# Another order on VectorE, GpSimd and ScalarE in a cross-attention and FFN kernel: maximum and residual earlier, statistics of x later

## What is computed

```python
x = x + xattn(layernorm(x), ctx, Wq, Wk, Wv, Wskip)   # einsum over channels, softmax over 256
x = x + ffn(layernorm(x), qweight, scales, zeros, bias)

# xattn: q = Wq up; k = Wk down; v = Wv down; energy = q^T k / sqrt(128)
#        x = softmax(energy) v^T; returns Wskip up + x
# ffn:   w = (nibbles - round(zeros / scales)) * scales; returns x w + bias   (1024 by 1024)
```

## Time and profile before

| what | value |
|---|---|
| median of 3 runs | 538.35 us (537.58 to 538.68) |
| profiled execution, its own time | 536.69 us |
| its span in the profile | 534.9 us |
| mean granted clock of TensorE | 0.987 |
| busy share of the span | PE 94%, DVE 80%, ACT 69%, POOL 82% |
| HBM traffic | 23.87 MB read, 16.78 MB written |
| DMA hardware queue's packets | 79.9% of 16 engines' span |

### The profile page before, as it was taken

One profiled execution on the slowest core, in us unless ns is written; L12 is line 12 of the kernel. 1 busy time (PEld: TensorE's weight loads), 2 busy tenths in 40 slices (PEclk: granted clock), 3 DMA queues, 4 the chain that ended last, 5 costly groups with the idle time before them and its releaser, 6 DMA issues.

```text
span 534.9 us, 9272 instructions
## 1 busy us (share of the span) xinstructions
PE 505.3 (94%) x2700; PEld 311.9 (58%) x2700; DVE 429.2 (80%) x980; ACT 369.7 (69%) x844; POOL 436.4 (82%) x651
## 2 busy tenths in 40 slices
PE   5657999999999999999999999999999999999976
PEld 4544565656666665666665656666665666665532
DVE  6898788889888888888888889888888888877631
ACT  4877777776777767677777776767767677776510
POOL 5998788889888888988888889888888988888751
PEclk9888999999999999999999999999999999999998
DMA  8636888898788898888898788888897888876852
GB/s 319 172 88 115 144 191 179 179 184 186 168 150 206 188 178 178 181 189 153 178 204 163 193 185 181 157 192 178 172 196 177 194 171 173 163 142 143 154 113 78
DMA packets 236787, 91.65 MB, mean 171 GB/s; under 512 B 219200, under 2 KB 223808, under 8 KB 236736
## 3 DMA queue, kind: packets, MB, share of 16 engines
q1 hardware_dynamic: 236016, 90.92, 79.9%
q10 hardware_dynamic: 720, 0.14, 0.1%
HBM read 23.87 MB, written 16.78 MB: 76 GB/s over the span
## 4 chain that ended last, share of the span: by engine, by line
POOL 44%; PE 29%; issue 12%; ACT 5%; DVE 5%; DMA 3%; SPq 1%; POOLq 0%; ACTq 0%
PE ps_y L907 14%; POOL sb_prob L255 10%; POOL sb_xc_lo L270 9%; POOL sb_xn_lo L297 9%; POOL sb_o L249 6%; PE ps_e L861 5%; PE ps_o L891 4%; ACT sb_xn L487 4%; POOL sb_nb L281 3%; PE ps_o L887 2%; POOL sb_rstd L279 2%; DMA sb_xnt_lo<-sb_xn_lo 2%; POOL sb_rstd L263 2%; PE ps_kv L872 1%; PE ps_y L911 1%
## 5 line engine op out<-in xcount | busy, mean ns | idle before, releaser
L907 PE MATMUL ps_y<-sb_wf,sb_xnt_hi 128*128 128x512 f16 x512 | 196.9, 385 | 7.4 <-DMA sb_xnt_lo<-sb_xn_lo 4.0
L907 PE MATMUL ps_y<-sb_wf,sb_xnt_lo 128*128 128x512 f16 x512 | 196.0, 383 | 0.0
L469 ACT ACTIVATE sb_prob<-ps_e,sb_neg_max 128x256 f32<-128x256 f32 x256 | 117.8, 468 | 53.2 <-DVE sb_neg_max L647 53.2
L255 POOL TENSOR_SCALAR sb_prob<-sb_prob,sb_rsum 128x256 f32<-128x256 f32 x256 | 122.8, 493 | 4.2 <-DVE sb_rsum L652 4.2
L656 DVE TENSOR_TENSOR sb_p_lo<-sb_prob,sb_p_hi 128x1024 f16<-128x1024 f32 x64 | 78.0, 1220 | 48.0 <-ACT sb_p_hi L478 48.0
L297 POOL TENSOR_TENSOR sb_xn_lo<-sb_xn,sb_xn_hi 128x512 f16<-128x512 f32 x64 | 76.0, 1206 | 44.0 <-ACT sb_xn_hi L496 44.0
L861 PE MATMUL ps_e<-sb_k_hi,sb_xc_hi 128*128 128x256 f32 x256 | 85.4, 334 | 10.1 <-DVE sb_k_lo L635 5.5
L907 PEld LDWEIGHTS ps_y<-sb_wf,sb_xnt_hi 128*128 128x128 f16 x512 | 50.2, 98 | 72.8 <-issue 14.1
L478 ACT ACTIVATE sb_p_hi<-sb_prob 128x1024 f16<-128x1024 f32 x64 | 67.3, 1052 | 34.4 <-issue 30.0
L249 POOL TENSOR_TENSOR sb_o<-sb_prod,sb_x 128x512 f32<-128x512 f32 x64 | 80.8, 1281 | 9.5 <-DVE sb_prod L690 9.5
L647 DVE TENSOR_REDUCE sb_neg_max<-ps_e 128x2 f32<-128x512 f32 x128 | 84.8, 681 | 1.6 <-PE ps_e L861 1.2
(11 more groups left out here) (113 smaller groups left out, 917.7 us busy)
## 6 DMA issues: line engine op xcount, KB each, us to landing
sb_x<-in_x_dram SPq DMA_DIRECT2D x32, 512.0 KB, 4.3
out_dram<-sb_o SPq DMA_DIRECT2D x64, 256.0 KB, 2.3
sb_ctx<-in_ctx_dram SPq DMA_DIRECT2D x32, 128.0 KB, 2.8
sb_q<-in_L_ffn_qweight_dram SPq DMA_DIRECT2D x4, 512.0 KB, 7.1
sb_seed_l<-sb_rs SPq DMA_DIRECT2D x96, 0.5 KB, 2.2
sb_pt_hi<-sb_p_hi SPq DMA_TRANSPOSE x64, 4.1
sb_pt_lo<-sb_p_lo SPq DMA_TRANSPOSE x64, 3.4
sb_scale_row<-in_L_ffn_scales_dram SPq DMA_DIRECT2D x1, 512.0 KB, 9.3
```

The source lines that it names most:

```text
L255: last = pool.tensor_scalar(prob[:, j, t, :], prob[:, j, t, :], rsum[:, j, t:t + 1], P_SCALE, ALU.mult, ALU.mult)
L469: done = act.activation(prob[:, j, t, :], ps_e[j % 2][:, t, :], ACT.Exp, bias=neg_max[:, j, t:t + 1], accum_out=esum[:, j, t:t + 1])
L907: pe.matmul(ps_y[h][:, :], xnt_p[s][:, par, kt, :], wf[:, kt, h * HALF:(h + 1) * HALF], start=kt == 0 and s == 0, stop=False)
```

## The change

DVE does the fourth row maximum and the second residual earlier: the two low parts of keys and values move behind the third inversion, both halves of the second statistics stand together behind the fourth maximum, and the first layer norm's statistics of x(m) move from the head of the step to just before the last `probs_lo`. In step 2 `seed_rows` moves ahead and `nibbles(3)` falls behind with `values_lo`. POOL gets `inverse_std2` ahead of the fourth normalisation as before, but the second half of the low centred x now comes behind that normalisation, and `inverse_std1(m)` after it. ACT does the last exponentials before the first half of `probs_hi`. The low centred x gets one semaphore for each half: PE's first scores wait for the first half alone, and the third chunk of scores for the second.

```diff
@@ gpsimd: centred_lo @@
-                last = pool.tensor_tensor(xc_lo[:, n % 3, cols], xc[:, cols], xc_hi[:, n % 3, cols].bitcast(F32),
-                                          ALU.subtract)
-                if h == HALVES - 1:
-                    last.then_inc(xclo_done, 1)
+                pool.tensor_tensor(xc_lo[:, n % 3, cols], xc[:, cols], xc_hi[:, n % 3, cols].bitcast(F32),
+                                   ALU.subtract).then_inc(xclo_done[h], 1)
@@ gpsimd: step @@
                 if ran(b):
                     normalise(b, 0)
+                if ran(n):
+                    centred_lo(n, 0)
+                if ran(b):
+                    normalise(b, 1)
+                    normalise(b, 2)
+                if ran(a):
+                    inverse_std2(a)
+                if ran(b):
+                    normalise(b, 3)
+                if ran(n):
+                    centred_lo(n, 1)
                 if ran(m):
                     inverse_std1(m)
-                if ran(n):
-                    centred_lo(n, 0)
-                if ran(b):
-                    normalise(b, 1)
-                    normalise(b, 2)
-                if ran(n):
-                    centred_lo(n, 1)
-                if ran(a):
-                    inverse_std2(a)
-                if ran(b):
-                    normalise(b, 3)
@@ scalar: step @@
                     exps(b, 2)
+                    exps(b, 3)
                     probs_hi(b, 0)
-                    exps(b, 3)
@@ vector: step @@
                     value_scale(n)
-                if ran(m):
-                    stats1(m, 0)
-                    stats1(m, 1)
-                    aggregate1(m)
                 if ran(b):
                     invert(b, 0)
-                if ran(m):
-                    variance1(m)
                 if ran(a):
                     residual(a, 0)
                 if ran(b):
                     row_max(b, 1)
                     row_max(b, 2)
+                if t == 2:
+                    seed_rows()
+                if ran(b):
+                    invert(b, 1)
+                if ran(a):
+                    residual(a, 1)
+                if ran(b):
+                    invert(b, 2)
+                    row_max(b, 3)
                 if ran(a):
                     stats2(a, 0)
-                if ran(b):
-                    invert(b, 1)
+                    stats2(a, 1)
+                    aggregate2(a)
+                if ran(b):
+                    invert(b, 3)
                 if ran(n):
                     keys_lo(n)
                     values_lo(n)
                 if t == 2:
                     nibbles(3)
-                    seed_rows()
-                if ran(b):
-                    invert(b, 2)
-                if ran(a):
-                    residual(a, 1)
-                if ran(b):
-                    row_max(b, 3)
-                if ran(a):
-                    stats2(a, 1)
-                    aggregate2(a)
-                if ran(b):
-                    invert(b, 3)
+                if ran(b):
                     probs_lo(b, 0)
                 if ran(m):
                     context_max(m)
                 if ran(q):
                     scale_product(q, 0)
+                if ran(m):
+                    stats1(m, 0)
+                    stats1(m, 1)
+                    aggregate1(m)
+                    variance1(m)
                 if ran(b):
                     probs_lo(b, 1)
@@ tensor: scores @@
+                if j == 2:
+                    pe.wait_ge(xclo_done[1], b + 1)
@@ tensor: keys_ready @@
                 pe.wait_ge(klo_done, b + 1)
-                pe.wait_ge(xclo_done, b + 1)
+                pe.wait_ge(xclo_done[0], b + 1)
```

More of the change, by code:

```diff
@@ L109, in xattn_ffn_program @@
         w_step, w_scaled, proj_done, proj_kept = sem("w_step"), sem("w_scaled"), sem("proj_done"), sem("proj_kept")
-        key_done, key_kept, k0_done, xchi0_done, xclo0_done = (sem(n) for n in ("key", "key_kept", "k0", "xchi0", "xclo0"))
+        key_done, key_kept, k0_done, xchi0_done = (sem(n) for n in ("key", "key_kept", "k0", "xchi0"))
         k1_done, recip_done = sem("k1"), sem("recip")
@@ L115, in xattn_ffn_program @@
         st1_done, mv1_done, ve1_done, rstd1_done = (sem(n) for n in ("st1", "mv1", "ve1", "rstd1"))
-        xc_done, xchi_done, xclo_done = (sem(n) for n in ("xc", "xchi", "xclo"))
+        xc_done, xchi_done, xclo_done = sem("xc"), sem("xchi"), sems("xclo", HALVES)
         amax_done, kv_done, t_step, kvhi_done, kvlo_done = (sem(n) for n in ("amax", "kv", "t_step", "kvhi", "kvlo"))
@@ L386, in step @@
                     normalise(b, 0)
-                if ran(m):
-                    inverse_std1(m)
                 if ran(n):
@@ L399, in step @@
                     normalise(b, 3)
+                if ran(n):
+                    centred_lo(n, 1)
+                if ran(m):
+                    inverse_std1(m)
                 if ran(a):
@@ L422, in centre @@
                 if ran(n, 1):
-                    act.wait_ge(xclo_done, n)
+                    act.wait_ge(xclo_done[1], n)
                 act.activation(xc[:, :], x_sb[:, n % 4, :], ACT.Identity, bias=mv1[:, 0:1],
@@ L627, in first_centred_lo @@
                 done = dve.tensor_tensor(xc_lo[:, 0, cols], xc[:, cols], xc_hi[:, 0, cols].bitcast(F32), ALU.subtract)
-                done.then_inc((xclo0_done, xclo_done)[h], 1)
+                done.then_inc(xclo_done[h], 1)
             def keys_lo(n):
@@ L915, in keys_ready @@
                 pe.wait_ge(klo_done, b + 1)
-                pe.wait_ge(xclo_done, b + 1)
+                pe.wait_ge(xclo_done[0], b + 1)
             def run_in():
-                pe.wait_ge(klo_done, 1)
-                pe.wait_ge(xclo0_done, 1)
+                keys_ready(0)
                 scores(0, 0)
@@ L925, in run_in @@
                 second_keys()
-                pe.wait_ge(xclo_done, 1)
                 scores(0, 2)
```

## The result

| | before | after |
|---|---|---|
| median of 7 runs each | 537.70 us (537.26 to 538.68) | 539.75 us (539.38 to 540.99) |
| ratio, 95% interval | | 1.0037 [1.0025, 1.0049] |
| profiled execution, its span | 536.69 us, 534.9 us | 540.99 us, 539.2 us |

What follows compares the result with a forecast made beforehand. PE's 15.37 us step was taken as the floor, beside POOL's 15.42 us loop costing 0.8 us. Step 2 +1.0, steady steps +3.4 and end +1.2 gave +5.6: median 538.35 to 543.9 us, range 538.9 to 549.5.

Steps and rivals of the forecast that it cites:

- Part 1: Steady steps, DVE's new order: `probs_lo(b,1)` ends about 1 us after next scores 0 start, delaying transposes; net +3.4 us.
- the nine stands: Steady steps with a long `xn_hi` transpose issue: PE waits 0 to 1.2 us each, 4.2 us in all.
- rival A: Long issues no longer fall on the transposes, no stands; only step 2 and end cost: +0.4 to +1.4 us, chance 0.14.
- part 4: Low centred x, semaphore by halves: PE's first scores need only the first half; 0 to -0.15 us.
- Part 2: POOL's new order, steady steps: 15.42 us loop gone, worth 0.8 us; `xn_lo` ready 3.3 to 4.1 us after scores 0.
- The hold of 0.2: Steady steps: POOL's normalisation holds DVE's `probs_lo(b,0)`, so `probs_lo(b,1)` ends 0.2 us later; 0 to 0.5 possible.
- Parts 3 and 4: ACT's last exponentials first: nothing, or up to 1 us a step if uncovered; semaphore by halves: 0 to -0.15 us.
- Part 5: Step 2: first FFN starts early, stands about 4.6 us, half clock falls where PE bounds; +1.0 us, bounds -0.15 and +1.7.
- Part 6: Last steps: `stats2` now stands in the second layer norm's chain, 0.6 us twice; +1.2 us, ends 0.6 and 1.6.
- Both ends: Step 2, where the half clock falls later, +1.0 us, and the last steps' longer layer norm chain, +1.2 us.

Runs made afterwards that it cites:

- the middle alone: Changed kernel with the new order in steps 3 to 30 only, old order in step 2 and from step 31: 535.74 us, ratio 0.9973.
- the ladder: New order in steps 3 to 30 (0.9973), then new end (1.0008), then step 2 (1.0037); other way, step 2 before the end: 0.9973, 1.0028, 1.0037.

## Why the prediction was wrong

- **Part 1, the steady steps: this step failed.** Forecast +3.4 net, measured -0.7 in the profile and -1.0 to -1.45 by the middle alone. Its first half held: `probs_lo(b,1)` ends at T'+1.04 (1.0 worked out, without the 0.2 taken for a hold). Its second half, the nine stands of 4.2 us in all, did not: PE lost 0.2 us. "In the nine steps with the long issue" took these issues as fixed to the string; they belong to 16 KB transfers of instructions, and the one PE wait that part 4 adds, whose effect on them was put at nothing, moved those out of the string. That is rival A's condition, word for word, held at 0.14. By the profiles this move is worth 1.3 us. The larger part of the error is the price: with the transfers left on the string the stands came to 1.5, not 4.2. 2.4 of the 4.2 were put on two steps, those of the stands at 345 us and behind it, because they "had no room at all". What had used up the room in the first was the drift of `probs_lo(b,1)` to T'+0.85 by POOL's loop, together with a landing of 4.10 us; in the second, where it ended at T'+0.16, it was a long issue with a landing of 4.01. Part 2 ends that drift, so part 1 counted a lateness that part 2 takes away and put its own microsecond on top. And in the changed kernel `xn_lo` lands within 3.6 us from sequence 3 to 28, and 0.4 us of each long issue is taken up by SP's pause.
- **The hold of 0.2.** DVE was not held: `probs_lo` takes 1.21 to 1.22 us in the steady steps. POOL was (the mean of its 256 normalisations went from 493 to 616 ns). The Trainium skill has this rule (SBUF — State Buffer, section Who interferes with whom): the pair of ports goes for a whole instruction to whoever issues first. The trace agrees in the length of the hold, and in the order for `inverse_std1`, which begins 0.16 us behind `probs_lo` and takes 1.46. In the other case it doesn't show the order: by the records the normalisation begins at 382.49, 0.06 us ahead of `probs_lo` (382.55), and is held all the same.
- **Part 2** was right in each statement: the loop gone, the wait for `ve1` in place of that for `xn_hi`, `xn_lo` ready at T'+4.1, the upper of its bounds. It was priced too low: 0.8 by the stands of one profiled execution, which was itself 1.0 us under its median. The middle alone won 1.45 and POOL's order alone 1.9, or 1.0 to 1.1 and 1.5 to 1.9 among runs of the same mean clock. What the rest over 0.8 is, stands that the profiled execution of before did not show or something else, is open.
- **Parts 3 and 4** cost nothing by themselves that the profile shows, but for what part 4 did to the transfers.
- **Part 5, step 2: mechanism right, term mis-sized.** +1.0 forecast, 1.3 to 1.6 by the ratios (3.0 on one way of the ladder), 2.9 in the profile. The bound of +1.7 assumed that the half clock lasts 3.4 us; it lasted 6.8 in the profiled execution after and 3.4 in four kernels with a like stand. At 3.4 it cost about 1.5, within the bound; at 6.8, 2.8. What makes the difference is open.
- **Part 6, the end: right** by the profile, +1.2 forecast and 1.4 (1.0 against the kernel with the old end) measured; the ratios give 0.5 to 1.9 and hardly bound it.
- **The sum.** Both ends together 2.2 forecast, 3.4 measured; the middle +3.4 forecast, -1.45 measured: 5.6 + 1.2 - 4.85 = 2.0, the result. That the sign came out right is luck in so far: the loss is that of the ends, not that of the part that carried the forecast. Rival A had the mechanism and nearly the sum (+0.4 to +1.4), with -0.8 in the middle.

## What to carry to other kernels

A long DMA issue that comes back every few steps has a cause of its own, and before it is added to a moved string it must be found: look at what else the queues carry in that stretch. When an engine's start is moved forward while its last input is not, the stand moves too, and with it the place where the clock is low; ask first whether the last input can come earlier, which here was worth more (4 us and more) than the whole reordering. And try each engine's order alone: here POOL's by itself gave 0.9964, and all three together 1.0037. Before a stand is added to a step that already had one, find out what made the first, and whether the change takes it away.

## What was not expected of the hardware

- A transfer of instructions of 16 KB that meets a DMA transpose of 256 KB makes its issue take up to 2.5 us instead of 1.23 to 1.28 (2.0 to 2.5 in most cases). The transfers keep to PE's count of instructions, and one satisfied wait more per step of PE is enough to move them through a step (nine long issues of one transpose to two).
- Behind a stand of 4.7 us of PE the clock was at half for 6.8 us in one execution and 3.4 in four others. With 32 idle matmuls in the stand it stayed at full.
- One-element operations on POOL are held as large ones are: 0.27 or 0.75 us, 0.54 or 1.46, by where DVE's two-input operation falls.
